# Attention stage of a conditioned two-layer block: a fifth pair buffer, second folds issued a pair later, sums ten tiles behind

## The reference

```python
B, N, D = hidden.shape            # 2, 2048, 512
hd = D // num_heads               # 16 heads of 32
h = _sln(hidden, w, ln_g, ln_b, Wg, bg, Wb, bb)
qkv = (h @ Wqkv.T + bqkv).reshape(B, N, num_heads, hd, 3)
energy = jnp.einsum('bhqd,bhkd->bhqk', q, k)
att = jax.nn.softmax(energy, axis=-1) / D ** 0.5
out = jnp.einsum('bhqk,bhkd->bhqd', att, v)
out = jnp.moveaxis(out, 1, 2).reshape(B, N, D)
out = out @ Wp.T + bp
h1 = out + hidden
h2 = _sln(h1, w, ln_g, ln_b, Wg, bg, Wb, bb)
return h2 + h1
```

## Time and profile before

| | |
|---|---|
| median of 3 runs | 2997.95 us (2995.87 to 3001.31) |
| the profiled execution | 2999.27 us, span 2997.5 us |
| mean granted TensorE clock | 0.984 |
| busy: PE, DVE, POOL, ACT | 2882.8, 2013.3, 1802.6, 1512.2 us |
| busy share: PE, DVE, POOL, ACT | 96%, 67%, 60%, 50% |
| attention, first to last instruction of its exponentials and sums | about 1290 to 2891 us |

### The profile page before, as it was taken

One profiled execution on the slowest core, in us unless ns is written; L12 is line 12 of the kernel. 1 busy time (PEld: TensorE's weight loads), 2 busy tenths in 40 slices (PEclk: granted clock), 3 DMA queues, 4 the chain that ended last, 5 costly groups with the idle time before them and its releaser, 6 DMA issues.

```text
span 2997.5 us, 41315 instructions
## 1 busy us (share of the span) xinstructions
PE 2882.8 (96%) x15018; PEld 1915.0 (64%) x15018; DVE 2013.3 (67%) x3559; ACT 1512.2 (50%) x2756; POOL 1802.6 (60%) x797
## 2 busy tenths in 40 slices
PE   4899999999999998999999999999999999999997
PEld 2787788888888886755555555555555555555456
DVE  6873332222233556678888888888888887888549
ACT  3552233232333222156666666666666666666654
POOL 2775310111110442158898899888899888989864
PEclk7999999999999999999999999999999999999999
DMA  6543100000001657486668866687766778666668
GB/s 213 174 142 127 43 29 0 29 29 28 29 29 43 212 206 226 171 192 127 138 138 181 185 137 141 129 192 157 165 134 132 165 166 172 138 136 129 148 194 290
DMA packets 155051, 405.64 MB, mean 135 GB/s; under 512 B 12102, under 2 KB 30506, under 8 KB 134343
## 3 DMA queue, kind: packets, MB, share of 16 engines
q0 software_dynamic: 22608, 164.64, 27.5%
q1 hardware_dynamic: 132248, 238.41, 26.0%
HBM read 144.51 MB, written 92.31 MB: 79 GB/s over the span
## 4 chain that ended last, share of the span: by engine, by line
POOL 21%; DMA 13%; PE 12%; issue 8%; DVE 2%; ACT 0%; POOLq 0%; SPq 0%; DVEq 0%; ACTq 0%
POOL pair L1947 19%; DMA pair<-pair 12%; PE psum L1724 3%; PE psum L1712 3%; PE psum L1697 3%; POOL v_out L1913 1%; DVE part_max L1833 1%; PE psum L1752 1%; POOL pair L1930 1%; DMA p_att_lo<-att_parts 1%; PE psum L37 1%; PE psum L39 1%; PE psum L38 1%; ACT probs L1803 0%; DVE p_h L2137 0%
## 5 line engine op out<-in xcount | busy, mean ns | idle before, releaser
L1833 DVE TENSOR_REDUCE part_max<-psum 128x1 f32<-128x512 f32 x1984 | 1213.6, 682 | 171.6 <-PE psum L1697 166.2
L1803 ACT ACTIVATE probs<-psum 128x512 f32<-128x512 f32 x2048 | 1046.1, 612 | 495.8 <-PE psum L1712 490.4
L1947 POOL TENSOR_TENSOR pair<-probs 128x2048 f32<-128x2048 f32 x255 | 1197.8, 4777 | 97.0 <-ACT probs L1803 78.9
L1712 PE MATMUL psum<-queries,keys 128*128 128x512 f32 x2048 | 839.3, 412 | 11.1 <-ACT probs L1803 5.4
L1697 PE MATMUL psum<-keys,queries 128*128 128x512 f32 x1984 | 796.1, 402 | 0.8
L1712 PEld LDWEIGHTS psum<-queries,keys 128*128 128x128 f32 x2048 | 383.7, 188 | 343.6 <-issue 215.0
L1724 PE MATMUL psum<-probs,values 128*32 128x512 f32 x4096 | 511.8, 600 | 0.0
L1697 PEld LDWEIGHTS psum<-keys,queries 128*128 128x128 f32 x1984 | 374.0, 189 | 92.1 <-DVE part_max L1833 43.1
L1077 DVE TENSOR_TENSOR h_lo<-w_stage,h_hi 128x512 fp32r<-128x512 f32 x128 | 100.7, 787 | 486.1 <-ACT h_hi L986 486.0
L979 ACT ACTIVATE w_stage<-psum,b_col 128x512 f32<-128x512 f32 x128 | 88.3, 690 | 483.2 <-PE psum L39 482.4
L1724 PEld LDWEIGHTS psum<-probs,values 128*32 128x32 f32 x4096 | 107.0, 109 | 242.1 <-ACT probs L1803 133.7
(11 more groups left out here) (337 smaller groups left out, 3708.7 us busy)
## 6 DMA issues: line engine op xcount, KB each, us to landing
pair<-pair POOLq DMA_DIRECT2D x157, 1024.0 KB, 7.4
queries<-q_parts SPq DMA_DIRECT2D x96, 256.0 KB, 6.3
keys<-k_parts SPq DMA_DIRECT2D x42, 512.0 KB, 10.7
s_x<-in_x_dram SPq DMA_DIRECT2D x8, 1024.0 KB, 7.8
s_y<-in_x_dram SPq DMA_DIRECT2D x8, 1024.0 KB, 5.5
y_rows<-s_y SPq DMA_DIRECT2D x8, 1024.0 KB, 4.7
q_parts<-qk_hi SPq DMA_DIRECT2D x32, 256.0 KB, 2.0
q_parts<-qk_lo SPq DMA_DIRECT2D x32, 256.0 KB, 2.3
```

Of the source, the lines that this page charges most:

```text
L1712: nc.tensor.matmul(psum[:, SC + unit % 3, :], keys[place(count)[0]][:, h, kt * P:(kt + 1) * P], queries[count % NQ][:, h, :], start=True, ...
L1803: act.activation(probs[tile % NPROB][:, h, :], psum[:, SC + unit % 3, :], ACT.Exp).then_inc(exp_ready, 1)
L1833: dve.tensor_reduce(part_max[:, h * TT + qt, kc:kc + 1], max_slot(), AX.X, ALU.max).then_inc(max_read, 1)
L1947: pool.tensor_tensor(pair[number % NPAIR][:, :, :], probs[2 * number % NPROB][:, :, :], probs[(2 * number + 1) % NPROB][:, :, :], ALU.add) ...
```

## The change

A fifth pair buffer is made from the space of the raw projection weight. The weight itself is loaded in block 30 instead, into a place that was `queries2` until block 29 and becomes `p_att_lo1` later; for that SP waits for its four transposes before `load_result(1)`. Pair n+5 now reuses the buffer of pair n. Second folds are issued behind the next pair's addition: fold 2 behind pair 3, fold 5 behind pair 6. Sums come 10 tiles behind the last pair: kt 15, and kt 5 and kt 9 of the next block; those of the last block stay 8 behind. On DVE the transpose of the sums moves from kt 9 to kt 11, and inverse and spread from kt 11 to kt 13, both ahead of a gather in the same tile. The slots of the weight's transposes in the ring are counted out for each of them.

```diff
-    NPROB, NPAIR, NQ = 6, 4, 3
+    NPROB, NPAIR, NQ = 6, 5, 3
-    AV_LAG, SUM_LAG = 3, 8
+    AV_LAG, SUM_LAG, LAST_LAG = 3, 10, 8
...
-    pair = [sb(f"pair{n}", [P, HG, CH]) for n in range(NPAIR)]
+    pair = [sb(f"pair{n}", [P, HG, CH]) for n in range(NPAIR - 1)] + [spare]
...
-    SUMMED_AT = {2 * group[-1] + 1 + SUM_LAG: g for g, group in enumerate(GROUPS[:DIRECT])}
+    SUMMED_AT = {2 * group[-1] + 1 + (SUM_LAG if group[-1] < PAIRS * (BLOCKS - 1) else LAST_LAG): g for g, group in enumerate(GROUPS[:DIRECT])}
     WP_AT = (BLOCKS - 1) * NKT + 3
-    WP_SLOT = (MAXES + 1) * (BLOCKS - 1) + sum(1 for tile in SUMMED_AT if tile <= WP_AT)
+    WP_SLOTS = [(MAXES + 1) * (BLOCKS - 1) + k + sum(1 for tile in SUMMED_AT if tile <= WP_AT + k) for k in range(KT)]
...
         load_values(0, 1)
-
-        sp.dma_start(wp[:, :, :], a["L1_cond_Wp"].rearrange("(m p) k -> p m k", p=P)).then_inc(wp_ld, 16)
...
                 ahead = count - (BLOCKS - B)
+                if ahead == 0:
+                    sp.dma_start(wp[:, :, :], a["L1_cond_Wp"].rearrange("(m p) k -> p m k", p=P)).then_inc(wp_ld, 16)
+                else:
+                    sp.wait_ge(wt_tp, KT)
                 sp.wait_ge(att_st, 32 * (BLOCKS - B * NCH + B * ahead + 2))
                 later["load_result"](sp, 0, ahead)
...
+            if count > 0 and kt == 11:
+                turn_sums(count - 1)
+            if count > 0 and kt == 13:
+                invert(count - 1)
+                spread_inverse(count - 1)
             if tile in SUMMED_AT:
                 gather(SUMMED_AT[tile])
-            if count > 0 and kt == 9:
-                turn_sums(count - 1)
-            if count > 0 and kt == 11:
-                invert(count - 1)
-                spread_inverse(count - 1)
...
-            if number in FOLDS:
+            if number in FOLDS and number - 1 not in FOLDS:
                 fold(number)
+            if number - 1 in FOLDS and number - 2 in FOLDS:
+                fold(number - 1)
...
+        first_columns = HG * L + 2 * HG * CH + HG * TT * NCH + 3 * 32 + 2 * D
+        with ExitStack() as last_blocks:
+            own = scope(last_blocks)
+            own("ahead_of_wp", [P, first_columns + OPERAND_STEP - HD + HG * L])
+            wp = own("wp_raw", [P, KT, D])
```

More of the change, by code:

```diff
@@ L1493, in qkv_stage, with attention_stage @@
     return {"sync": sync, "tensor": tensor, "scalar": scalar, "vector": vector, "gpsimd": gpsimd}
-def attention_stage(nc, sb, sem, psum, a, ident, wp, later, first, q_dram, k_dram, v_dram, att_dram):
+def attention_stage(nc, sb, sem, psum, a, ident, spare, wp, later, first, q_dram, k_dram, v_dram, att_dram):
     R = 3 * HD
@@ L1808, in scalar @@
                 act.wait_ge(wt_tp, k + 1)
-                act.activation(later["wt_hi"][:, k, :], psum[:, MX + (WP_SLOT + k) % NMX, :], ACT.Copy).then_inc(whi_ready, 1)
+                act.activation(later["wt_hi"][:, k, :], psum[:, MX + WP_SLOTS[k] % NMX, :], ACT.Copy).then_inc(whi_ready, 1)
         copy_out(BLOCKS - 1)
@@ L1958, in banks_read @@
     def banks_read(engine):
-        engine.wait_ge(max_read, WP_SLOT + KT + len(GROUPS) - sum(1 for tile in SUMMED_AT if tile <= WP_AT))
+        engine.wait_ge(max_read, (MAXES + 1) * (BLOCKS - 1) + KT + len(GROUPS))
         engine.wait_ge(o_copied, BLOCKS + 1)
@@ L2341, in cond_seq_kernel @@
         nc.all_engine_barrier()
+        first_columns = HG * L + 2 * HG * CH + HG * TT * NCH + 3 * 32 + 2 * D
[3 more added lines that the diff above has]
+            wp = own("wp_raw", [P, KT, D])
         with ExitStack() as block_0:
-            scope(block_0)("first_tiles", [P, HG * L + 2 * HG * CH + HG * TT * NCH + 3 * 32 + 2 * D])
+            scope(block_0)("first_tiles", [P, first_columns])
             later = {}
             with ExitStack() as stage:
-                four = attention_stage(nc, scope(stage), sem, psum, a, ident, raw_weight, later, first, q_dram, k_dram, v_dram, att_dram)
+                four = attention_stage(nc, scope(stage), sem, psum, a, ident, raw_weight, wp, later, first, q_dram, k_dram, v_dram, att_dram)
         with ExitStack() as stage:
```

## The result

The changed kernel takes 2973.94 us (median of 4 runs, 2969.37 to 2975.36), the kernel before beside it 2998.48. The ratio is 0.9918, with a 95% interval of 0.9906 to 0.9929: 0.82% faster, 24.5 us. The sign was forecast. The size was not: 2985 was forecast, with a range that ended at 2978. Two more sets of runs of the same changed kernel gave 2972.04 and 2975.14 us, ratios 0.9912 and 0.9924.

A forecast was written before the change was run, and what follows sets the result against it. It took attention as bound by PE's steady rate, plus rare fold DMA stalls and a small DVE stall in every block. 2999.27 - 12.6 + 2 - 4.4 + 1 = 2985.3, called 2985 us; range 2978 to 2995.

The forecast's parts named there:

- part 2: DVE's order: DVE starts about 0.26 us earlier after kt 11, 0.25 late after kt 13; together taken as 0.
- this bound (-8): DVE's order: only the earlier start after kt 11 counts, over 30 blocks, -8 us; the opposite bound was +7.5.
- Part 1: Folds and sums in attention: later sums and later second folds remove 12.6 us of stalls, with 2 us left over.
- residue of 2: Attention blocks: 2 us of PE's stalls for folds kept as remaining, out of 12.6 us removed.
- 1 us to spare in the worst case: Worst fold 2, behind 1.5 MB of keys: needed at 2479.8, expected through by about 2479.
- Part 3: Projection weight, loaded in block 30 instead of at the start: 4.4 us less there, 1 us left over; start 0.
- residue of 1 for the fourth MB: Block 30: 1 us kept against the 4.4 us gain, the weight's load joining 3 MB of projection loads.
- A: Rival: fold 5 meets queries, keys and values, 1 to 1.5 us late six times; 8 us back, about 2993; chance 0.12.
- the head start protects little: Folds issued ahead of a load burst: transfers of all issuing engines interleave on 16 DMA engines, so leaving first helps little.
- B: Rival: fold 5 lasts over 15.4 us in every block, PE waits 29 times; 3014 at 1 us each; chance 0.04.
- D: Rival: stalls only move, sums wait as before, the end's gain eaten by the fourth MB; 2997; chance 0.06.
- C: Rival: DVE's shift costs 0.25 us in 29 blocks without the 0.26 gain, 7 us; 2992; chance 0.08.

## Why the prediction was wrong, step by step

**The step that failed is in part 2**: "there DVE starts the following pair at about 1.02 instead of 0.77, 0.25 late. Together nothing; I take 0." Its first half was right: leaving kt 11 shortens the pair of kt 12 and 13 by 0.29 us (7.15 to 6.86 alone, 6.30 to 6.01 with the folds), and both directions were run. The second half failed twice. DVE came 0.89 us after PE, not 1.02: the reciprocal starts at 1483.55, 0.08 before the recorded end of the reductions ahead of it (1479.95 + 3.68). And I took a late start as passed on to PE "almost one for one", while a start of 0.89 costs nothing: the pair lasts 6.59, as other pairs with a sum do (6.60). So the term was not 0 but -8.4 in 28 blocks of the first trace, -6.4 in those of two later traces of the same kernel (28 x 49.17 against 1370.4), and -8.3 by medians. I had named exactly this bound (-8) and then called +-3 the likelier width because both halves came from the same rows; the lower end of the range allowed for 0.2 us a block. With the whole bound kept, and neither residue, the range would have reached down to about 2974 (2985.3 - 8 - 2 - 1), which is about the measured time.

**Part 1 was right in its mechanism and 2 us too dear.** Stalls of 12.6 went entirely; no residue of 2 was left. The reason for the residue, 1 us to spare in the worst case, was wrong: fold 2 of block 23 took 10.4 us from issue to landing instead of 15.8 to its sum, and landed 6.5 us before its sum. It now leaves 5.2 us behind the first of the keys (2448.57 against 2443.33), where it had left 3.2 behind (2462.95 against 2459.80); that this distance is what made it shorter was not tested. That the sums' lag and the later issue carry it, and not the buffer by itself, is shown. With DVE's new order throughout, the medians are: sums 8 behind and folds at once 2994.0, second folds later 2985.8, sums 10 behind 2982.2, both 2972.0. (The first two are of the second group, the last two of the first; the kernel before had 2997.05 and 2997.75 there.) The later issue is worth 8 to 10 us and the later sums 12 to 14. I had given the later issue no sum of its own. POOL's 82.0 us of waiting are free in quiet blocks, as I wrote. With second folds at once, the 10 us lie in the four blocks named above (50.00, 49.66, 50.34 and 49.87 us, 4.4 above quiet ones) and in blocks 30 and 31 (48.18 and 52.83, 6.0 more than in the changed kernel).

**Part 3 had the right sum and the wrong fold.** 4.4 less was forecast for blocks 30 and 31, 3.9 is measured between the two traces, and the residue of 1 for the fourth MB was nothing. But I had fold 4 take 12.7 + 3.2 = 15.9 us beside 4 MB. It takes 8.6, and it leaves ahead of the loads. So it is in all traces with the later second folds: the first load leaves 0.66 to 0.71 us behind fold 4, which takes 8.5 or 8.6 us (9.7 with sums 8 tiles behind). In the four traces with second folds at once the first load leaves at the same instant or up to 0.93 us ahead of fold 4, and that takes 12.2 to 13.8 us. So the price that I took for the burst depends on who leaves first, and a POOL that is on time sends the fold first. The start gained nothing that stands out of the scatter of the first copy.

**The sum:** 2985.3 - 2 - 8.4 - 1, and +0.5 for block 31, gives 2974.4, against 2973.94 measured. Term by term it is 12.6 + 8.4 + 3.9 = 24.9 less, and the medians are 24.5 apart (2998.48 to 2973.94). That this comes so close is partly luck: the 12.6 are the stalls of a single trace of the kernel before, and with the DVE term of the later traces the sum is 2 us less.

**The rivals.** A: two folds of a block did get longer. Fold 5 takes 8.9 us in the median instead of 8.3, and fold 7, which now leaves while fold 5 and the queries are still under way, 10.3 instead of 7.4 (7.1 in the changed kernel with second folds at once); the queries' loads take 9.5 instead of 6.3. The others are as before (7.0 to 7.3 against 7.1 to 7.3), fold 4 too, though it leaves 7 us behind fold 2. But no sum waited. That transfers under way together lengthen each other, whoever issued them, agrees with the rule of the Trainium skill that I quoted (page "DMA: Bandwidth & Descriptors", section "Issuing engines are not separate DMA queues"). My own step from it, that "the head start protects little", does not hold for fold 4 of block 30: 0.66 us of head start, and 8.6 us instead of 12.2 to 13.8. B and D did not happen. C was the right place with the wrong sign.

## What to carry to other kernels

When work moves between two places on a helper engine, price both from how late the bound engine can bear it, and measure that tolerance: here 0.12 us beyond the ordinary start were free and 0.40 us were not, and it decided 6 to 8 us. A wait on an engine with slack is free only until the next burst; the gain of issuing something a step later appears in the disturbed blocks, not in the quiet one that is easiest to read. If a bound can only be narrowed by an argument from few rows, keep the bound in the range.

## What was not expected of the hardware

The records of DVE's instructions overlap at their ends: eight reductions of 0.68 us take 4.84 to 4.88 in all, and a reciprocal starts 0.08 us before the recorded end of the six reductions ahead of it. A wait for the negation's own end followed by a semaphore step costs 0.21 us of DVE from start to start (0.41 against 0.20), and leaving it out shortened the pair by 0.15 us on PE (6.01 to 5.86).

An adding DMA of 1 MB takes 7.0 to 7.3 us from issue to landing where little else is under way, 10.3 in the median where the one before it and 0.75 MB of queries are, and 13.9 and 15.8 us until its sum starts beside key loads. Who leaves first mattered in these traces: leaving 0.66 us ahead of 4 MB of loads such a DMA took 8.6 us, leaving 0.17 us behind the first of them 13.1.
